# The last stage of an attention and expert layer: loops written out, and rows gathered four tiles ahead in place of eight

## Chip, cores and metric

The kernel runs on one core of a Trainium2 chip. The metric is the device time of one execution in microseconds (us); the time shown for a kernel is the median of several runs. One further execution was recorded by the hardware profiler, and the rows below come from it.

## What is computed

A layer norm of `x` (2 x 2048 x 512, float32) feeds two branches whose results are added to `x`. One is attention with 16 heads and a latent of 128; the other sends each token to 2 of 8 experts and takes the mean of their two results.

```python
x = L0_attn_x                                   # (2, 2048, 512)
xn = _layernorm(x, axis=-1)
x = x + attn(xn, ...) + ffn(xn, ...)
# attn ends with: out = o @ Wo.T + bo           (o: heads side by side, after Wo_h)
# ffn:
gate_logits = jnp.einsum('nsd,de->nse', x, gate_w) + gate_b
_, top_idx = jax.lax.top_k(gate_logits, K)      # K = 2 of E = 8
all_out = jax.nn.relu(jnp.einsum('nsd,edo->nseo', x, expert_w) + expert_b)
sel = jnp.take_along_axis(all_out, top_idx[..., None], axis=2)
return sel.mean(axis=2)
```

## The kernel before

The program is written engine by engine: SyncE, GpSimd (POOL), ScalarE (ACT), VectorE (DVE) and TensorE (PE) each have a list of instructions, and semaphores alone set the order between them. A helper `count(n)` adds 4 to a count because most semaphores start at 4.

The stages are: weights folded together; layer norm, queries, keys, values and gate logits, tile by tile (a tile is 128 tokens, `NT` = 32 tiles); attention, two heads per turn of a loop; then the experts. The tokens are sorted by expert into `PT` = 72 tiles of rows. For each, POOL gathers the token rows, PE multiplies them with the chosen expert's weights, DVE adds the biases, and SyncE writes the result to a table in device memory, `y_dram` (called `expert_rows` in the trace).

The last stage begins when the 72 expert tiles are done. It works on the 32 token tiles in order. Tile `n` uses slot `q = n % 8` of a ring of `OUT_RING` = 8 slots; each slot has one PSUM bank `PS[:, q]`, one residual buffer `xc[q]`, two buffers for gathered rows `y_g[q][0]` and `y_g[q][1]`, and one result buffer `acc[q]`. In the trace `y_g` is called `w_hi` or `w_lo` and `acc` `w_lo`, after the memory that they reuse, and `xc` is called `arena`.

- PE, `project` (line 1457): 12 matmuls (4 blocks of rows times 3 products of fp16 halves) give the attention output of one tile in bank `q`. The first 8 tiles are straight code; tiles 8 to 31 run in a loop of 3 turns with 8 tiles in the body. From tile 8 on it waits until DVE has read the same bank's previous tile.
- POOL (lines 739 to 749): straight code before and after. It waits until the whole expert table is written, then makes two indirect DMAs per tile, 128 rows of 512 float32 each (line 746), from the table into `y_g[q]`. For `n >= 8` the pair waits for `acc_done` of tile `n - 8`.
- DVE, `sums` (lines 1199 to 1208): a loop of 4 turns with 8 tiles in the body. It waits for the slot's previous result to be out (`out_done`, line 1202), for the residual (`xc_in`, line 1203), for the projection (`proj_ps`, line 1204), and adds projection and residual (line 1205); it waits for the gathered rows (`yg_in`, line 1206) and adds the two (lines 1207 and 1208). The last of these raises `acc_done`.
- SyncE: `result` (line 543) waits for `acc_done` and writes 128 x 512 float32 out; `residual` (line 537) loads `xc[q]` for the tile eight further on. The residual loads of tiles 0 to 7 are issued during the expert stage. A loop of 3 turns holds 8 results and 8 loads; the results of tiles 24 to 31 are straight code.

All instructions of a loop that name tile `m * 8 + q` take their addresses and counts from registers, which further register instructions fill.

Of the kernel before, what the change touches and what calls it, by code (L numbers as in the profile page):

```python
# [7 lines left out]
def layer_kernel(nc, x, Wq, Wdkv, Wuk, Wuv, ln_g, ln_b, Wo_h, Wo, bo,  # L8
# [30 lines left out]
    NT = B * ST  # L39
# [21 lines left out]
    with ctx:  # L61
# [3 lines left out]
        def sem(name):  # L65
            return ctx.enter_context(nc.semaphore(name))
# [32 lines left out]
        def carve(arena):  # L99
            at = [0]  # L100

            def take(n, dt=f32):
# [85 lines left out]
        tD = carve(arena2)  # L188
        xg_T = [tD(2 * KB * P, f16).rearrange("p (z k c) -> p z k c", z=2, k=KB) for _ in range(2)]
        y_sb = [tD(E) for _ in range(2)]  # L190
        OUT_RING = 8
        xc = [tD(E) for _ in range(4)]
        x_ahead = [tD(E).bitcast(f16) for _ in range(2)]
        xc += [tD(E) for _ in range(2)]
# [3 lines left out]
                 for w in (w_hi, w_lo) for q in range(NE * KB * E // (2 * E))]  # L198
        y_g, acc = [spare[TOP * q:TOP * (q + 1)] for q in range(OUT_RING)], spare[TOP * OUT_RING:TOP * OUT_RING + OUT_RING]
        x_g = [x_g0[:, :]] + x_ahead  # L200
# [3 lines left out]

        OUT_SEMS = [f"{name}{q}" for name in ("xc_in", "out_done", "yg_in") for q in range(OUT_RING)]
        s = {n: sem(n) for n in (
# [23 lines left out]
        START = 4  # L230
        FROM_ZERO = ["id_zero", "id_done", "ids_in", "xg_in0", "xg_in1", "xg_in2", "xg_in3"] + OUT_SEMS[-OUT_RING:]

        def count(n):

            return n + START
# [136 lines left out]
        def _(sp):  # L374
# [161 lines left out]
            def residual(m, q):  # L536
                sp.dma_start(xc[q], xc_v[q % B][ds(m * (OUT_RING // B) + q // B, 1)].rearrange("t p d -> (t p) d")
                             ).then_inc(s[f"xc_in{q}"], 16)

            def result(m, q):  # L540
                sp.wait_ge(s["acc_done"], count(m * OUT_RING + q + 1))
                sp.sem_inc(s["step_at"], 1)
                sp.dma_start(out_v[q % B][ds(m * (OUT_RING // B) + q // B, 1)].rearrange("t p d -> (t p) d"), acc[q]
                             ).then_inc(s[f"out_done{q}"], 16)

            def expert_rows(i):
                for u in range(2):
                    sp.wait_ge(s["y_done"], count(i * 2 + u + 1))
                    sp.dma_start(y_dram[ds((i * 2 + u) * P, P), :], y_sb[u]).then_inc(s[f"y_st{u}"], 16)
# [10 lines left out]
                residual(0, q)  # L560
            with sp.Fori(BESIDE + 5 + OUT_RING, PT // 2) as i:
                expert_rows(i)
            with sp.Fori(0, NT // OUT_RING - 1) as m:
                for q in range(OUT_RING):
                    result(m, q)
                    residual(m + 1, q)
# [7 lines left out]
        def _(pool):  # L574
# [165 lines left out]
                pool.wait_ge(s[f"y_st{u}"], count(16 * PT // 2))  # L740
            for n in range(NT):
                q, at = n % OUT_RING, n // B + n % B * ST
                if n >= OUT_RING:
                    pool.wait_ge(s["acc_done"], count(n - OUT_RING + 1))
                for k in range(TOP):
                    g.indirect_dma_start(out=y_g[q][k], out_offset=None, in_=y_dram,  # L746
                                         in_offset=bass.IndirectOffsetOnAxis(ap=place[:, k, at:at + 1], axis=0)
                                         ).then_inc(s[f"yg_in{q}"], 16)
# [154 lines left out]
        def _(dve):  # L903
# [264 lines left out]
            for it in range(ROUTING_ITS):  # L1168
                for kk in SPAN:
                    heads(it, True, [kk])  # L1170
                    if kk % 2 == 0:
                        n = next(steps)
# [26 lines left out]
            def sums(m, q):  # L1199
                n = m * OUT_RING + q  # L1200
                lnk, cnt = linker(dve, s["dveE"], n * 2)
                dve.wait_ge(s[f"out_done{q}"], count(m * 16))
                dve.wait_ge(s[f"xc_in{q}"], count((m + 1) * 16))
                dve.wait_ge(s["proj_ps"], count(n + 1))
                lnk(v.scalar_tensor_tensor(out=acc[q], in0=PS[:, q, :], scalar=1.0 / WS, in1=xc[q], op0=ALU.mult, op1=ALU.add))
                dve.wait_ge(s[f"yg_in{q}"], (m + 1) * (16 * TOP))
                lnk(v.tensor_tensor(acc[q], acc[q], y_g[q][0], ALU.add))
                v.tensor_tensor(acc[q], acc[q], y_g[q][1], ALU.add).then_inc(s["acc_done"], 1)

            with dve.Fori(0, NT // OUT_RING) as m:  # L1210
                for q in range(OUT_RING):
                    sums(m, q)

# [2 lines left out]
        def _(pe):  # L1216
# [234 lines left out]
            def project(m, q, again):  # L1451
                u, at = q % B, q // B * P
                if again:
                    pe.wait_ge(s["dveE"], count((m * OUT_RING + q - OUT_RING) * 2 + 1))
                terms = [(k, z, y) for k in range(KB) for z, y in pairs]
                for q_, (k, z, y) in enumerate(terms):
                    last = t.matmul(PS[:, q, :], attnT[:, u * KB + k, ds(m, 1), z, at:at + P].rearrange("p o q -> p (o q)"),  # L1457
                                    comb_hl[:, y, k, :], start=q_ == 0, stop=q_ == len(terms) - 1)
                last.then_inc(s["proj_ps"], 1)

            for q in range(OUT_RING):
                project(0, q, False)
            with pe.Fori(1, NT // OUT_RING) as m:
                for q in range(OUT_RING):
                    project(m, q, True)

# [24 lines left out]
```

## Time and profile before

| | us |
|---|---|
| median of 3 runs | 1613.08 |
| lowest and highest | 1612.5, 1616.36 |
| the profiled execution | 1613.21 |
| its span, first to last instruction | 1611.5 |
| PE busy | 1512.8 (94%) |
| DVE busy | 1137.4 (71%) |
| ACT busy | 902.2 (56%) |
| POOL busy | 583.6 (36%) |

Times within a profile are counted from the start of the span. A timeline row reads: start, duration, engine, source line, operation, what it writes and reads, how many instructions were merged, and in brackets how long the engine sat idle before it and what released it; "issue" means that nothing which the profile shows was waited for, "remote" that no releasing instruction of the trace was found. PEld is PE's weight load, an engine name ending in q its sequencer (register, branch and DMA-issuing instructions).

### The profile page before, as it was taken

What the parts mean: (1) busy time and instruction counts of PE and PEld (TensorE: products, weight loads), DVE (VectorE), ACT (ScalarE), POOL (GpSimd) and SP (SyncE); (2) the same over time, 40 slices, a digit from 0 to 9 for tenths busy, and PEclk for the clock granted to TensorE, in tenths of its full rate; (3) what the DMA queues carried; (4) which work ended last, traced back from release to release, by engine and by line L of the source; (5) the groups of instructions that cost most, each with busy time, mean ns of one, the idle gap of its engine ahead of it and who ended that gap; (6) DMA issues with size and microseconds to landing.
All of it is one profiled execution on the core that took longest, in us unless ns stands there. A gap on an engine that the chain in (4) does not pass through costs nothing.

```text
span 1611.5 us, 44000 instructions
## 1 busy us (share of the span) xinstructions
PE 1512.8 (94%) x12544; PEld 809.9 (50%) x12545; DVE 1137.4 (71%) x2384; ACT 902.2 (56%) x1629; POOL 583.6 (36%) x788
## 2 busy tenths in 40 slices
PE   5799989999999999999999999999999899999697
PEld 2788844444444444454444444444444455555233
DVE  5788778887777777777777777777777244444366
ACT  1677746666666666666666666666666433332000
POOL 2444402323454454432232223222322543332653
PEclk9899979999999999999999999999999999999798
DMA  6588851223222322233223322232232466554787
GB/s 161 164 268 271 236 151 52 72 67 93 71 69 62 90 77 70 64 83 84 70 63 81 85 70 63 81 86 70 63 78 63 135 207 217 177 174 142 253 280 250
DMA packets 161456, 198.05 MB, mean 123 GB/s; under 512 B 45792, under 2 KB 95072, under 8 KB 161024
## 3 DMA queue, kind: packets, MB, share of 16 engines
q1 hardware_dynamic: 125088, 117.11, 24.9%
q10 hardware_dynamic: 23328, 44.60, 9.4%
q0 software_dynamic: 12992, 35.77, 7.4%
q8 instruction: 21, 0.34, 0.1%
q14 instruction: 27, 0.22, 0.0%
HBM read 109.13 MB, written 63.12 MB: 107 GB/s over the span
## 4 chain that ended last, share of the span: by engine, by line
PE 79%; DVE 8%; issue 5%; DMA 3%; SPq 2%; ACT 1%; POOL 1%; DVEq 0%; ACTq 0%; POOLq 0%
PE PS L1328 29%; PE PS L1383 28%; PE PS L1433 12%; PE PS L1457 5%; DVE pm L1122 4%; PE PS L1415 2%; DMA arena<-in_x 1%; SPq L423 1%; DVE mx L1127 1%; SPq L415 1%; DVE mx L1126 1%; DVE arena L988 0%; PE PS L1274 0%; DMA q_pieces<-w_hi 0%; DMA arena<-in_Wuv 0%
## 5 line engine op out<-in xcount | busy, mean ns | idle before, releaser
L1122 DVE TENSOR_REDUCE pm<-PS 128x1 f32<-128x512 f32 (+3 forms) x1280 | 717.0, 602 | 200.3 <-PE PS L1328 185.3
L871 ACT ACTIVATE arena<-PS 128x512 f32<-128x512 f32 (+1 forms) x1152 | 613.5, 574 | 300.0 <-PE PS L1328 277.9
L1328 PE MATMUL PS<-arena 97*64 97x512 f16 (+7 forms) x5120 | 693.5, 353 | 26.6 <-DVE pm L1122 20.3
L1383 PE MATMUL PS<-arena 128*33 128x512 f32 (+3 forms) x2560 | 634.7, 531 | 1.9 <-POOL arena L649 1.9
L1328 PEld LDWEIGHTS PS<-arena 96*64 96x64 f16 (+1 forms) x5120 | 329.3, 110 | 416.3 <-DVE pm L1122 140.1
L649 POOL TENSOR_SCALAR_AFFINE_SELECT arena<-arena 128x256 f32<-128x256 f32 (+1 forms) x256 | 111.5, 436 | 546.7 <-ACT arena L871 545.6
L1383 PEld LDWEIGHTS PS<-arena 128*33 128x33 f32 x2560 | 159.4, 111 | 81.5 <-POOL arena L649 2.6
L1433 PE MATMUL PS<-w_hi,arena 128*128 x576 | 172.5, 381 | 0.7 <-issue 0.7
L890 ACT ACTIVATE arena<-PS 128x1024 f16<-128x1024 f32 x72 | 73.8, 1024 | 143.5 <-PE PS L1415 141.4
L1328 PE MATMUL PS<-later,deny 128*64 128x128 f16 x1024 | 145.4, 222 | 0.0
L1186 DVE SCALAR_TENSOR_TENSOR arena<-PS,eb_bc 128x512 f32<-128x512 f32 x72 | 49.8, 692 | 114.8 <-PE PS L1433 111.3
L1457 PE MATMUL PS<-comb_hl,arena 128*128 128x512 f16 x384 | 94.1, 400 | 22.9 <-issue 22.7
L1433 PE MATMUL PS<-w_lo,arena 128*128 x288 | 109.9, 382 | 0.0
L880 ACT ACTIVATE arena<-PS 97x512 f32<-97x512 f32 x128 | 76.5, 597 | 57.7 <-PE PS L1383 40.9
L1328 PEld LDWEIGHTS PS<-later,deny 128*64 128x64 f16 x1024 | 75.9, 112 | 57.1 <-issue 23.7
L746 POOL DMA_INDIRECT w_hi<-expert_rows,place x64 | 65.7, 1026 | 55.1 <-DMA expert_rows<-arena 21.7
L674 POOL TENSOR_TENSOR w_hi<-x_g,ws_col 128x512 f32 (+1 forms) x32 | 33.5, 1048 | 135.4 <-DVE bv_bc L1143 135.4
L1433 PEld LDWEIGHTS PS<-w_hi,arena 128*128 128x128 f16 x576 | 53.6, 98 | 53.0 <-issue 2.5
L1457 PEld LDWEIGHTS PS<-comb_hl,arena 128*128 (+1 forms) x384 | 38.4, 101 | 78.6 <-issue 40.0
L638 POOL DMA_INDIRECT token_of_place<-token_id,place_at x64 | 63.1, 986 | 16.4 <-issue 15.2
L688 POOL DMA_INDIRECT arena<-xn_rows,cur_id x54 | 52.6, 975 | 43.8 <-POOL cur_id L685 39.8
L621 POOL TENSOR_TENSOR arena<-arena 128x512 f16<-128x512 f32 x32 | 37.4, 1170 | 70.2 <-ACT arena L786 70.2
(174 smaller groups left out, 1296.8 us busy)
## 6 DMA issues: line engine op xcount, KB each, us to landing
expert_rows<-arena SPq DMA_DIRECT2D x72, 256.0 KB
comb_hl<-arena SPq DMA_DIRECT2D x256, 64.0 KB
arena<-q_pieces ACTq DMA_DIRECT2D x90, 128.0 KB
arena<-k_pieces ACTq DMA_DIRECT2D x90, 128.0 KB
v_rows<-w_lo SPq DMA_DIRECT2D x8, 1056.0 KB, 7.5
arena<-in_x SPq DMA_DIRECT2D x16, 512.0 KB, 5.7
xn_rows<-arena SPq DMA_DIRECT2D x16, 512.0 KB, 6.1
q_pieces<-w_hi SPq DMA_DIRECT2D x32, 256.0 KB, 5.3
```

Source lines behind the costliest of these rows:

```text
L638: g.indirect_dma_start(out=id_dram, out_offset=bass.IndirectOffsetOnAxis(ap=place_at[:, k, i:i + 1], axis=0), in_=token_id[:, i:i + 1], in ...
L649: g.affine_select(out=both[:, :, 0:wm], in_=both[:, :, 0:wm], compare_op=ALU.is_ge, fill=nought, base=0, pattern=[[step, 2], [1, wm]], cha ...
L688: g.indirect_dma_start(out=x_g[q], out_offset=None, in_=xn_dram, in_offset=bass.IndirectOffsetOnAxis(ap=cur_id[:, q:q + 1], axis=0)).then_ ...
L746: g.indirect_dma_start(out=y_g[q][k], out_offset=None, in_=y_dram, in_offset=bass.IndirectOffsetOnAxis(ap=place[:, k, at:at + 1], axis=0)) ...
L871: a.activation(probs[kk % 4][:, a_ * CH:a_ * CH + w], PS[:, s2_bank(k, x), 0:w], ACT.Exp, scale=SCALE).then_inc(s["exp_done"], 1)
L880: a.activation(ot[q % 2][0:2 * HD + V1, :], PS[0:2 * HD + V1, 6 + q % 2, :], ACT.Copy).then_inc(s["ot_done"], 1)
L890: a.activation(xg_T[u].rearrange("p z k c -> p (z k c)"), PS[:, 4 + 2 * u:6 + 2 * u, :].rearrange("p z c -> p (z c)"), ACT.Copy).then_inc( ...
L1122: v.reduce_max(pm[:, c, r, p:p + 1], PS[:, S1_BANK[n], 0:w], AX).then_inc(s["s1_done"], 1)
L1328: last = t.matmul(PS[h:h + P // 2, bank, cols], lhsT[:, h:h + P // 2], rhs, start=start, stop=stop)
L1383: last = t.matmul(PS[rows_, 6 + c % 2, CH - wds[a]:CH], v_sb[pu % 2][:, j + a, :], probs[pk % 4][:, a * off:a * off + wds[a]], start=p_ in ...
L1433: last = t.matmul(PS[:, u, :], xg_T[u][:, z, k, :], w[:, ds(e, 1), k * E:(k + 1) * E].rearrange("p e c -> p (e c)"), start=q_ == 0, stop=q ...
L1457: last = t.matmul(PS[:, q, :], attnT[:, u * KB + k, ds(m, 1), z, at:at + P].rearrange("p o q -> p (o q)"), comb_hl[:, y, k, :], start=q_ = ...
```

## The change

Two things change. On SyncE, DVE and PE the three loops of the last stage become Python loops, so that all 32 tiles (24 on PE, after the 8 that were straight already) are written out with constant addresses and counts. And a new constant `GATHERS_AHEAD` = 4 takes the place of the ring's 8 in POOL's wait: the gathers of tile `n` now wait for the sums of tile `n - 4`, from tile 4 on. Rings, buffers, transfers and arithmetic stay.

```diff
-        OUT_RING = 8
+        OUT_RING, GATHERS_AHEAD = 8, 4
@@ SyncE
-            with sp.Fori(0, NT // OUT_RING - 1) as m:
+            for m in range(NT // OUT_RING - 1):
                 for q in range(OUT_RING):
                     result(m, q)
                     residual(m + 1, q)
@@ POOL
             for n in range(NT):
                 q, at = n % OUT_RING, n // B + n % B * ST
-                if n >= OUT_RING:
-                    pool.wait_ge(s["acc_done"], count(n - OUT_RING + 1))
+                if n >= GATHERS_AHEAD:
+                    pool.wait_ge(s["acc_done"], count(n - GATHERS_AHEAD + 1))
                 for k in range(TOP):
                     g.indirect_dma_start(out=y_g[q][k], out_offset=None, in_=y_dram,
@@ DVE
-            with dve.Fori(0, NT // OUT_RING) as m:
+            for m in range(NT // OUT_RING):
                 for q in range(OUT_RING):
                     sums(m, q)
@@ PE
             for q in range(OUT_RING):
                 project(0, q, False)
-            with pe.Fori(1, NT // OUT_RING) as m:
+            for m in range(1, NT // OUT_RING):
                 for q in range(OUT_RING):
                     project(m, q, True)
```

## Rows read from the trace of the kernel before

**Rows 1.** The page: busy tenths of TensorE in 40 equal slices of the span.
```profile
PE   5799989999999999999999999999999899999697
```

**Rows 2.** Groups of instructions, 1488 to 1612: xcount, busy, mean ns, idle before, releasers.
```profile
L746 POOL DMA_INDIRECT w_hi<-expert_rows,place x64 | 65.7, 1026 | 55.1 <-DMA expert_rows<-arena 21.7 <-issue 19.2 <-DVE w_lo L1208 14.2
...
L1205 DVE SCALAR_TENSOR_TENSOR w_lo<-PS,arena 128x512 f32<-128x512 f32 x32 | 21.9, 685 | 42.0 <-remote 35.3 <-PE PS L1457 6.7
```

**Rows 3.** Timeline of TensorE in the last stage.
```profile
1488.44 21.62 PE L1457 MATMUL PS<-comb_hl,arena 128*128 128x512 f16 x98 [0.94 <-issue]
...
1531.70 0.58 PE L1457 MATMUL PS<-comb_hl,arena 128*128 128x512 f16 x1 [2.21 <-issue]
1533.11 18.12 PE L1457 MATMUL PS<-comb_hl,arena 128*128 128x512 f16 x71 [0.82 <-issue]
...
1553.71 16.78 PE L1457 MATMUL PS<-comb_hl,arena 128*128 128x512 f16 x77 [0.36 <-issue]
...
1576.48 28.02 PE L1457 MATMUL PS<-comb_hl,arena 128*128 128x512 f16 x116 [1.71 <-issue]
```

**Rows 4.** Timeline of VectorE: tiles 0, 2, then 6, 8, 12, 19, 25.
```profile
1498.67 0.69 DVE L1207 TENSOR_TENSOR w_lo<-w_lo,w_hi 128x512 f32<-128x512 f32 x1 [6.75 <-DMA w_hi<-expert_rows,place]
...
1506.27 0.69 DVE L1207 TENSOR_TENSOR w_lo<-w_lo,w_hi 128x512 f32<-128x512 f32 x1 [2.77 <-DMA w_hi<-expert_rows,place]
...
1533.86 0.69 DVE L1205 SCALAR_TENSOR_TENSOR w_lo<-PS,arena 128x512 f32<-128x512 f32 x1 [14.86 <-remote]
...
1537.97 0.69 DVE L1205 SCALAR_TENSOR_TENSOR w_lo<-PS,arena 128x512 f32<-128x512 f32 x1
...
1553.70 0.69 DVE L1205 SCALAR_TENSOR_TENSOR w_lo<-PS,arena 128x512 f32<-128x512 f32 x1 [6.46 <-remote]
...
1577.24 0.69 DVE L1205 SCALAR_TENSOR_TENSOR w_lo<-PS,arena 128x512 f32<-128x512 f32 x1 [8.94 <-remote]
...
1594.29 0.69 DVE L1205 SCALAR_TENSOR_TENSOR w_lo<-PS,arena 128x512 f32<-128x512 f32 x1 [4.54 <-PE PS L1457]
```

**Rows 5.** Stretches: length, busy and xcount of PE, PEld, DVE, ACT, POOL; PEclk, DMA share, GB/s.
```profile
1520.00:1532.00 12.00, 3.23 (x6) 0.62 (x6) 0.00 (x0) 0.00 (x0) 7.93 (x9) 0.50 0.88 282
1536.00:1544.00 8.00, 8.00 (x34) 3.42 (x33) 7.63 (x12) 0.00 (x0) 6.21 (x6) 0.88 0.79 258
1544.00:1552.00 8.00, 7.60 (x34) 3.05 (x32) 2.39 (x4) 0.00 (x0) 6.17 (x7) 1.00 0.99 367
```

**Rows 6.** Timeline of SyncE's queue: results out.
```profile
1500.32 0.69 SPq L543 DMA_DIRECT2D out<-w_lo  x1
...
1525.33 0.71 SPq L543 DMA_DIRECT2D out<-w_lo  x1
...
1536.25 0.33 SPq L543 DMA_DIRECT2D out<-w_lo  x1
```

**Rows 7.** Timeline of GpSimd: the first gather, those after a pause, the last.
```profile
1494.00 0.95 POOL L746 DMA_INDIRECT w_hi<-expert_rows,place  x1 [21.70 <-DMA expert_rows<-arena]
...
1536.27 0.95 POOL L746 DMA_INDIRECT w_hi<-expert_rows,place  x1 [5.89 <-DVE w_lo L1208]
...
1556.36 0.95 POOL L746 DMA_INDIRECT w_hi<-expert_rows,place  x1 [4.02 <-DVE w_lo L1208]
...
1579.65 0.95 POOL L746 DMA_INDIRECT w_hi<-expert_rows,place  x1 [4.26 <-DVE w_lo L1208]
...
1592.13 0.95 POOL L746 DMA_INDIRECT w_hi<-expert_rows,place  x1 [0.30 <-issue]
```

**Rows 8.** Single lines, TensorE's sequencer: ns min/median/max, first and last start.
```profile
L1457 PEldq FUSED_REGOPS  x192: 46/46/46, 1505.6 to 1600.0; - x192
...
L1463 PEldq COMPARE_BRANCH  x3: 76/207/209, 1553.9 to 1600.6; - x3
```

**Rows 9.** DMA queues between 1540 and 1544: kind, packets, MB, share of 16 engines.
```profile
q8 instruction: 1, 0.02, 1.7%
```

## Prediction

> **What bounds the kernel now.** I read the page first: TensorE (PE) is busy at 9 tenths in nearly every slice, but in the last three, where the touched stage lies, it has 6, 9 and 7 [rows 1]. Everything ahead keeps its time, so the sum is over that stage, from 1488.44 us, when the first projection matmul starts, to the end of the span at 1611.5.
>
> Then the stage by engine [rows 2]. Tiles are counted from 0. 32 tiles take four resources: PE 384 matmuls, in the straight part 98 of them in 21.62 us [rows 3], so some 2.65 us a tile and 85 us in all. VectorE (DVE) three operations a tile; its starts 1533.86 and 1537.97 are two tiles apart, so 2.06 us each and 66 us in all [rows 4]. GpSimd (POOL) two gathers a tile: 65.7 us busy and 19.2 us of gaps between them make 84.9 us, 1.33 us each [rows 2]. DMA 64 gathers, 32 results and 24 residual loads of 256 KB each, 31.5 MB; the fullest stretch moved 367 GB/s at a share of 0.99, which makes 86 us [rows 5]. So four floors lie between 66 and 86 us, and the stage takes 123.
>
> Where is the rest? DVE sat 42.0 us before its first sum of a tile, 35.3 of them "remote", and POOL 14.2 us behind DVE [rows 2]. In order of time: tile 6's first sum starts at 1533.86 after 14.86 us idle, tile 12's at 1553.70 after 6.46, tile 19's at 1577.24 after 8.94, tile 25's, which the trace puts down to PE, at 1594.29 after 4.54 [rows 4]. Of its waits (the ring's result out, the residual in, the projection) the first is met at once for tile 6 and the residual was loaded long ago; the projection is left. Yet PE had issued 98 matmuls by 1510.06, and tile 6 is complete with the 84th [rows 3]. From 1511 on PE issues a matmul every 1.4 or 2.1 us, 13 of them until 1531.70, though it waits for nobody ("issue"), and from 1533.11 it runs again, in the same moment as DVE [rows 3, 4]. SyncE's issues take 0.69 to 0.71 us each in this stretch and 0.33 after it [rows 6]. I read this as one thing, a **slow spell**: every instruction of PE and SyncE passes at one in some 0.7 us, and what PE has finished reaches DVE late. The lag is the same each time: 98 + 13 = 111 matmuls begun by 1531.7 against 84 released; 111 + 71 = 182 by 1551.2 against the 156 that tile 12 needs at 1553.70; 384 - 116 = 268 before 1576.48 against 240 for tile 19. That is 26 to 28 matmuls, over two tiles, and it explains why a spell is not felt at once.
>
> When do spells begin and end? They end when POOL stops: its pauses begin at 1530.4, 1552.3 and 1575.4 (start less idle time) and its last gather ends at 1593.1, and DVE is let go at 1533.86, 1553.70, 1577.24, 1594.29, that is 1.2 to 3.5 us later [rows 4, 7]. POOL stops only because its ring of 8 tiles is full: it had gathered tiles 0 to 13 and tile 14 wants the sum of tile 6. So the 14.86 us stall is long because POOL may run eight tiles ahead of a stalled DVE. Between 1520 and 1532 DVE did nothing at all, and the DMA share was still 0.88 [rows 5]. I can't show what a spell is, only its beginning under gathers and its end with them.
>
> **The change part by part.** (1) POOL waits for tile n-4 in place of n-8: the gathers of tiles 4 to 7 gain a wait too. POOL has nothing else queued, so only gathers stand behind it; DVE waits for those. Outside spells it costs nothing: a gather pair lands 2.5 to 4.9 us after its issue (at 1.25 us each from 1494.00, tile 0's pair is issued by 1496.2 and used at 1498.67, tile 2's by 1501.4 and used at 1506.27) [rows 4, 7]. Wait, two gathers, landing and two sums are 2.66 + 4.9 + 1.4 = 9.0 us for four tiles, 2.25 a tile, under POOL's own 2.66. If a landing took over 6.6 us this cover would be gone.
>
> In the first spell POOL may now go to tile 9, once tile 5 is summed, at 1519.0 (1533.86 less 14.86). With 28 gathers from 1494.00 to 1530.4, 1.3 us each, its 19th would be ready near 1517.4 to 1518; so 1.0 us idle, and the 20th ends by 1521.5. Then it waits for tile 6. The spell ends 1.2 to 3.5 us behind the gathers, as above, so at 1522.7 to 1525.0; with 2.1 us for tile 6's sums POOL restarts at 1524.8 to 1527.1. I take 4.2 us idle of 3.3 to 5.6. PE resumes some 10 us sooner than before.
>
> After it the same thing recurs. DVE ran 6, 7 and 6 tiles from one stall to the next (6, 12, 19, 25), and the lag of 26 to 28 matmuls in it doesn't depend on the ring. So I expect stalls near 12, 18 and 25, each with POOL idle for 4.0 to 5.9 us (three rows: 5.89, 4.02, 4.26 [rows 7]); I take 4.2 again.
>
> The ledger of POOL, before: 1494.0 + 84.9 + 14.2 = 1593.1, and a tail of 18.4 us to 1611.5, because seven tiles (25 to 31) were gathered and not summed: 7 x 2.06 after 1594.29, is 1608.7, then the last result's way out to 1611.5, 2.7 us. After: 1494.0 + 84.9 + 1.0 + 4.2 + 3 x 4.2 = 1596.7; the tail is short, since at most four tiles can be unsummed: landing 2.5 to 4.9 (3.7), two sums 1.4, way out 2.7, so 7.8 us. End of span 1604.5. So POOL is idle 3.6 us longer and the tail is 10.6 us shorter: **minus 7.0 us**. What is late next is POOL, then a stalled DVE.
>
> (2) The loops written out. PE loses 8 register instructions a tile (192 x 46 ns = 8.8 us), but a loop stretch had 77 matmuls in 16.78 us, 0.218 each, the straight part 98 in 21.62, 0.221: hidden, so nothing [rows 3, 8]. Three branches on PE are 76 to 209 ns each, 0.6 us at most, and at each PE is tiles ahead of DVE [rows 8]. DVE's tile keeps three operations of 0.69 us (685 ns the first; three such are 2.06, and 2.06 is its pitch), so its register steps are hidden; I take 0 [rows 2, 4]. SyncE loses a register step and a move for each of 48 transfers; if they take 0.7 us each in a spell, as its issues do [rows 6], results and residual loads leave up to 2.8 us a tile sooner there. Nobody waits for them (a residual is wanted eight tiles later), but more traffic falls into the spell. Taken at 0, with 0 to +1 us for each of four spells.
>
> Does straight code have to be fetched? An instruction packet came between 1540 and 1544 [rows 9], and PE was busy 8.00 of 8.00 us from 1536 to 1544 [rows 5]: that one cost nothing. The Trainium skill ("Runtime: NRT & Kernel Launch", section "Instruction fetch mechanics") says that code is streamed ahead in order and that a taken branch to a page outside the window makes the engine wait for a fetch, and so it speaks for writing loops out. The branches here show nothing of such a wait: DVE goes from tile 6 over the loop's end to tile 8 at its usual pitch. By that rule the loops' removal could only gain; by the row it gains nothing, and the sum has nothing of it.
>
> Sum: 1611.5 - 7.0 = 1604.5 for the span. The profiled execution took 1613.21, 1.7 more than its span and 0.1 over the median 1613.08. **Forecast 1606.2.**
>
> **The rivals.** *Spells rarer or gone.* Before, DVE left a stall with a full ring and ran at 2.06 us a tile, faster than POOL gathers: 0.5 MB of results and residuals in that time, beside the gathers, and the share reached 0.99 in 1544 to 1552 [rows 5]. With four tiles in hand it soon falls to POOL's 2.66. Against it: the first spell is there with DVE at POOL's pace (SyncE's issue took 0.69 us at 1500.32 already [rows 6]). With no spell: 1494.0 + 84.9 + 7.8 = 1586.7, time 1588.4; with two of four left, some 1597. Chance 0.20.
>
> *The gain given back.* If spells outlast the gathers by the 3.5 us of the first one rather than 1.2, or a fifth comes near tile 29, POOL's idle grows: four pauses of 5.9 in place of 4.2 add 6.8 us, so 1613; one further spell adds 4 to 6. Chance 0.15, times 1609 to 1616. This is also the case in which the change does nothing that it seems to: the new wait then only moves idle time from DVE to POOL.
>
> *Slower: code that comes late.* Straight code is new to PE, DVE and SyncE at each step, where the loop bodies were run again from what was there. Its packets queue with gathers at a DMA share of 0.9 and more. If they are not asked for early enough, each costs up to a landing, 4.9 us. PE's code of the stage grows from 16 tiles (8 straight, 8 in the loop) to 32, DVE's fourfold; I estimate 3 to 5 more packets from that, 15 to 25 us, less 7. It decides from 12 us (three late ones) upward: 1618 to 1624, 1621 in the middle. For: the DMA traffic; against: the packet of 1540 to 1544, and that a stalled engine also lets the queues drain. Chance 0.13.
>
> **How the numbers follow.** My forecast has 0.52, with a range of its own of 1600 to 1611 (idle 3.3 to 5.6 at the first, 4.0 to 5.9 at the others, landing 2.5 to 4.9, a spell less by luck). The measurement tells apart about 0.3%, 4.8 us, so bounds 1608.2 and 1617.9. Of the 0.52, 0.36 lies below 1608.2. Faster 0.36 + 0.20 = 0.56; same 0.16 + 0.11 = 0.27; slower 0.04 + 0.13 = 0.17. The range 1589 to 1616 leaves out the late code (0.13) and a few hundredths at either end of the others.
>
> **What would show it.** Right: DVE's "remote" wait before tile 6 ends at 1523 to 1525, not 1533.9; POOL shows four pauses behind DVE of 4 to 6 us in place of three, the last gather starts near 1596, the last sum follows it by 5 us, and SyncE's issues still take 0.7 us in stretches. Spells gone: no "remote" waits, DMA near 350 GB/s throughout. Late code: PE or DVE idle with "issue" while SyncE's issues are short, and instruction packets at these places. The forecast is wrong in its mechanism if a spell does not end with POOL's pause, or if pauses come every two or three tiles.

## The result, and the profile after

| | before | changed |
|---|---|---|
| median, us | 1613.24 (4 runs) | 1602.56 (4 runs) |
| lowest to highest | 1612.5 to 1616.36 | 1600.42 to 1605.32 |
| profiled execution: time, span | 1613.21, 1611.5 | 1605.32, 1603.6 |

The ratio is 0.9929, 95% interval 0.9911 to 0.9947: 11 us faster, on that chip. Which chip this first comparison ran on is not noted; on the chip of the next four experiments the kernel before takes 1612.9 us (22 runs), so the two are taken to be one, the **first chip**. On two other chips, met later by chance, the kernel before takes 1589 to 1591 us by itself, and no kernel timed beside it there differs from it by more than 0.1%; the changed kernel itself was not timed on them. The experiments come to that.

The page of the changed kernel, busy tenths of TensorE, answers [rows 1]: the last three slices are 8, 8 and 7.

```profile
PE   5799989999999999999999999999999999999887
```

The groups of the stage, from 1480 us to the end (answer to [rows 2]; busy and mean, then idle before and releasers):

```profile
L746 POOL DMA_INDIRECT w_hi<-expert_rows,place x64 | 66.0, 1031 | 54.5 <-DMA expert_rows<-arena 21.6 <-issue 18.0 <-DVE w_lo L1208 14.9
...
L1207 DVE TENSOR_TENSOR w_lo<-w_lo,w_hi 128x512 f32<-128x512 f32 x32 | 22.1, 692 | 20.7 <-DMA w_hi<-expert_rows,place 17.4 <-issue 2.7
L1205 DVE SCALAR_TENSOR_TENSOR w_lo<-PS,arena 128x512 f32<-128x512 f32 x32 | 21.9, 684 | 23.9 <-remote 21.2 <-PE PS L1457 2.7
```

DVE's "remote" waits fell from 35.3 to 21.2 us. POOL's pauses behind DVE didn't fall: 14.9 after 14.2. The timeline of DVE shows where its waits are now, at tiles 6, 7, 17 and 26 (answer to [rows 4]; before, they were at 5, 6, 12, 19 and 25):

```profile
1521.23 0.69 DVE L1205 SCALAR_TENSOR_TENSOR w_lo<-PS,arena 128x512 f32<-128x512 f32 x1 [4.61 <-remote]
...
1527.66 0.69 DVE L1205 SCALAR_TENSOR_TENSOR w_lo<-PS,arena 128x512 f32<-128x512 f32 x1 [4.29 <-remote]
...
1558.96 0.69 DVE L1205 SCALAR_TENSOR_TENSOR w_lo<-PS,arena 128x512 f32<-128x512 f32 x1 [6.05 <-remote]
...
1587.35 0.69 DVE L1205 SCALAR_TENSOR_TENSOR w_lo<-PS,arena 128x512 f32<-128x512 f32 x1 [6.27 <-remote]
```

The timeline of TensorE (answer to [rows 3]): long runs of matmuls, and between them single ones or a few at a time, some 0.3 to 1.1 us apart with nothing waited for.

```profile
1490.63 23.47 PE L1457 MATMUL PS<-comb_hl,arena 128*128 128x512 f16 x108 [0.94 <-issue]
...
1516.14 0.38 PE L1457 MATMUL PS<-comb_hl,arena 128*128 128x512 f16 x1 [1.05 <-issue]
...
1526.08 26.78 PE L1457 MATMUL PS<-comb_hl,arena 128*128 128x512 f16 x119 [0.37 <-issue]
...
1558.84 23.31 PE L1457 MATMUL PS<-comb_hl,arena 128*128 128x512 f16 x100 [0.33 <-issue]
```

What these "remote" waits wait for stands in the trace too, among its semaphore events, though the timeline names no releaser. `proj_ps` is the count that the last matmul of each tile raises. In the kernel before it is raised at 1533.83, 1533.96 and 1534.08 us, three times within 0.26 us, at the end of the stall of tile 6, and again three times in 0.25 to 0.27 us from 1553.67, 1577.22 and 1594.27. In the changed kernel the threes begin at 1527.53, 1558.84 and 1587.23. Three tiles are 36 matmuls, and one takes 0.216 us where they run on, so the last two of the three were multiplied earlier: their signals were held back and came out together. On the chips without such stalls `proj_ps` is raised every 2.59 us. (The traces of the first chip hold 22 to 30 of 33 of its events, those of the others all, so no signal's delay is measured by itself.)

The timeline of GpSimd (answer to [rows 7]): the first gather, the first one after each pause, the last one.

```profile
1496.10 0.94 POOL L746 DMA_INDIRECT w_hi<-expert_rows,place  x1 [21.61 <-DMA expert_rows<-arena]
...
1523.64 0.94 POOL L746 DMA_INDIRECT w_hi<-expert_rows,place  x1 [1.20 <-DVE w_lo L1208]
...
1530.07 0.95 POOL L746 DMA_INDIRECT w_hi<-expert_rows,place  x1 [4.23 <-DVE w_lo L1208]
...
1561.37 0.94 POOL L746 DMA_INDIRECT w_hi<-expert_rows,place  x1 [4.62 <-DVE w_lo L1208]
...
1589.77 0.94 POOL L746 DMA_INDIRECT w_hi<-expert_rows,place  x1 [4.83 <-DVE w_lo L1208]
...
1594.00 0.95 POOL L746 DMA_INDIRECT w_hi<-expert_rows,place  x1 [0.31 <-issue]
```

So the ledger of POOL (first gather, plus busy time and gaps between gathers, plus pauses behind DVE, plus the tail from its last gather to the end of the span) reads 1496.1 + 84.0 + 14.9 + 8.6 = 1603.6, against 1494.0 + 84.9 + 14.2 + 18.4 = 1611.5 before. The stage began 2.1 us later in this execution; counted from the first gather it is 10.0 us shorter, and 9.8 of that is the tail. This profiled execution is the slowest of the four, 2.8 us over their median.

### The profile page after: what moved, and what is told of

Its sections match the earlier page's. It is cut to its first block, busy times and chain, and to the rows that moved or that the text cites. A ratio compares the mean times of both kernels' runs of the same rounds, so it can differ in the third digit from the quotient of the medians.

```text
span 1603.6 us, 43541 instructions
## 1 busy us (share of the span) xinstructions
PE 1514.2 (94%) x12544; PEld 811.6 (51%) x12545; DVE 1136.6 (71%) x2384; ACT 902.1 (56%) x1629; POOL 583.4 (36%) x788
## 4 chain that ended last, share of the span: by engine, by line
PE 78%; DVE 9%; issue 4%; DMA 4%; SPq 2%; ACT 1%; POOL 1%; another core or an unknown queue 0%; DVEq 0%; ACTq 0%; POOLq 0%
PE PS L1328 28%; PE PS L1383 28%; PE PS L1433 12%; PE PS L1457 5%; DVE pm L1122 5%; PE PS L1415 2%; DMA arena<-in_x 1%; DVE mx L1127 1%; DMA q_pieces<-w_hi 1%; SPq L423 1%; SPq L415 1%; DVE mx L1126 1%; DVE arena L988 0%; PE PS L1274 0%; DMA bv_bc<-inverses 0%
## 5 line engine op out<-in xcount | busy, mean ns | idle before, releaser
L1328 PEld LDWEIGHTS PS<-arena 97*64 97x64 f16 (+1 forms) x5120 | 330.1, 110 | 417.5 <-DVE pm L1122 136.0
L674 POOL TENSOR_TENSOR w_hi<-x_g,ws_col 128x512 f32 (+1 forms) x32 | 33.5, 1047 | 137.0 <-DVE bv_bc L1143 137.0
L1457 PEld LDWEIGHTS PS<-comb_hl,arena 128*128 128x128 f16 x384 | 38.5, 101 | 68.8 <-issue 29.3
```

Source lines behind the costliest of these rows:

```text
L1328: last = t.matmul(PS[h:h + P // 2, bank, cols], lhsT[:, h:h + P // 2], rhs, start=start, stop=stop)
```

## The experiments

The first question was which half of the change brings the gain. Theory A is the prediction's: a spell lasts as long as POOL gathers, so the depth of its lead is all. Theory B is that the register and branch instructions of the loops are what is slow.

**One part alone: four ahead, loops kept.**

```diff
 # before.py
-        OUT_RING = 8
+        OUT_RING, GATHERS_AHEAD = 8, 4
-                if n >= OUT_RING:
-                    pool.wait_ge(s["acc_done"], count(n - OUT_RING + 1))
+                if n >= GATHERS_AHEAD:
+                    pool.wait_ge(s["acc_done"], count(n - GATHERS_AHEAD + 1))
```

> The loops stay, only the gathers wait for tile n-4. Theory A (the forecast's: a slow spell lasts as long as the gathers run, the ring's depth decides how long, loops cost nothing): the whole gain is here, 1600 to 1605 us, tile 6's first sum starts near 1523 and not 1534, four pauses of GpSimd. Theory B (the register and branch instructions of the loops are what is slow in a spell): little gain, 1610 to 1613.

Measured: 1605.9 us, ratio 0.9955 (0.9938 to 0.9972), so 7.0 us of the gain. The first row is the group of gathers, then DVE's timeline with the waits of 4 us and more, at tiles 5, 11, 18 and 24:

```profile
L746 POOL DMA_INDIRECT w_hi<-expert_rows,place x64 | 66.7, 1042 | 55.6 <-DMA expert_rows<-arena 20.8 <-issue 18.0 <-DVE w_lo L1208 16.8
```

```profile
1517.68 0.69 DVE L1205 SCALAR_TENSOR_TENSOR w_lo<-PS,arena 128x512 f32<-128x512 f32 x1 [7.08 <-remote]
...
1537.56 0.69 DVE L1205 SCALAR_TENSOR_TENSOR w_lo<-PS,arena 128x512 f32<-128x512 f32 x1 [4.56 <-remote]
...
1560.43 0.69 DVE L1205 SCALAR_TENSOR_TENSOR w_lo<-PS,arena 128x512 f32<-128x512 f32 x1 [5.04 <-PE PS L1457]
...
1580.37 0.69 DVE L1205 SCALAR_TENSOR_TENSOR w_lo<-PS,arena 128x512 f32<-128x512 f32 x1 [5.35 <-remote]
```

This is the forecast's picture: stalls 6 or 7 tiles apart, four pauses of POOL of 4.0 to 4.4 us (16.8 in all), and a tail of 8.5 us (1492.0 + 84.7 + 16.8 = 1593.5, span 1602.0). The stall of 14.86 us is gone. The median is 0.9 us above A's 1600 to 1605 and 4 below B's 1610 to 1613, and it isn't the whole gain, as A had it: nearer to A, but neither.

**The other part alone: straight code, eight ahead.**

```diff
 # after.py
-        OUT_RING, GATHERS_AHEAD = 8, 4
+        OUT_RING, GATHERS_AHEAD = 8, 8
```

> All loops written out, but the gathers wait for tile n-8 as before. Theory A: as before within 3 us, 1610 to 1615, with a stall of VectorE of some 15 us at tile 6 or 7 and a tail of some 18 us behind the last gather. Theory B: most of the gain, 1601 to 1606.

Measured: 1607.6 us, ratio 0.9966 (0.9953 to 0.998), 5.3 us faster. Neither theory had that. A's shape is there (a stall of 13.34 us at tile 7, a tail of 1609.5 - 1590.9 = 18.6 us), but the median is 2.4 us below A's range: with eight ahead, straight code is worth about 5 us on this chip. With four ahead it is worth 3.3 to 3.7 (1605.9 less 1602.6 or 1602.2). The group shows pauses of 11.5 us where the loops had 14.2, and DVE's timeline the long stall. This profiled execution is the slowest of eleven (1611.2 us), so it shows less of the gain than the median:

```profile
L746 POOL DMA_INDIRECT w_hi<-expert_rows,place x64 | 65.3, 1020 | 51.2 <-DMA expert_rows<-arena 21.1 <-issue 18.6 <-DVE w_lo L1208 11.5
```

```profile
1538.30 0.69 DVE L1205 SCALAR_TENSOR_TENSOR w_lo<-PS,arena 128x512 f32<-128x512 f32 x1 [13.34 <-remote]
```

The two parts alone give 7.0 and 5.3 us, together 10.7 against the 12.3 of their sum; with intervals of plus or minus 2 to 3 us on each, that they add up is not excluded.

**Other depths, straight code.**

```diff
 # after.py
-        OUT_RING, GATHERS_AHEAD = 8, 4
+        OUT_RING, GATHERS_AHEAD = 8, 3      # the other kernel: 8, 6
```

> Straight code, gathers wait for tile n-3. Theory A: spells end sooner, but two gathers (2.6), landing (up to 4.9) and two sums (1.4) make 9 us for three tiles, 3.0 a tile against 2.6 of GpSimd's own, so VectorE waits for rows: 1600 to 1610, about the time of four ahead. If landing is nearer 2.5 than 4.9 there is no such wait and the time is 1598 to 1601. Theory B: the same time as four ahead, 1602.

> Straight code, gathers wait for tile n-6. Theory A: half way between eight and four: the first stall ends some 5 us later than with four (GpSimd runs two tiles further), the tail is up to two tiles longer: 1605 to 1609. Theory B: 1602, no dependence on the depth.

Measured: three ahead 1602.9 us, ratio 0.9933 (0.9912 to 0.9954); six ahead 1607.5, ratio 0.9966 (0.9954 to 0.9979). Depth 3 and 4 are the same, 6 and 8 are the same (1607.5 and 1607.6), with the step between 4 and 6. Theory B, for which the depth is nothing, is out; for three ahead both theories allowed the time. For six ahead the profiled execution suggests why: its last long stall came at tile 26, when POOL had done everything, so the tail was 17.5 us (1494.1 + 83.6 + 10.9 = 1588.6, span 1606.1). Three ahead is the telling one. Its groups, then TensorE's timeline after 1520 us:

```profile
L746 POOL DMA_INDIRECT w_hi<-expert_rows,place x64 | 65.3, 1020 | 54.6 <-DMA expert_rows<-arena 21.1 <-issue 18.9 <-DVE w_lo L1208 14.6
L1207 DVE TENSOR_TENSOR w_lo<-w_lo,w_hi 128x512 f32<-128x512 f32 x32 | 22.2, 694 | 41.1 <-DMA w_hi<-expert_rows,place 36.3 <-issue 4.1 <-DVE w_lo L1205 0.3
L1205 DVE SCALAR_TENSOR_TENSOR w_lo<-PS,arena 128x512 f32<-128x512 f32 x32 | 21.9, 684 | 2.3 <-PE PS L1457 2.3
```

```profile
1520.66 54.55 PE L1457 MATMUL PS<-comb_hl,arena 128*128 128x512 f16 x252 [0.59 <-issue]
```

No "remote" wait is left, and 252 matmuls run through at 0.216 us each. Yet the time is that of four ahead, because POOL now pauses nine times for 0.8 to 2.7 us, 14.6 us in all, and DVE waits 36.3 us for rows. The spells' cost was turned into the cost of a lead too short for the landing time, at the same price.

These kernels also show that POOL's stop is what ends a spell. In straight code the first spell ends, that is TensorE's next long run of matmuls begins, 25.9 us after the first gather with three ahead, 30.0 and 33.5 with four (two profiled executions), 36.3 with six and 42.0 with eight. Each time it is 1.6 to 3.6 us after POOL has begun to wait for the first time.

**Which loop?** The next kernels were to tell apart TensorE's loop from the others', and its register instructions from its branches, and whether less traffic ends the spells.

```diff
 # f1_pe_straight: after.py with the loops of SyncE and VectorE put back
 # f2_pe_loop: after.py with TensorE's loop put back
 # f3_straight_regs: after.py with
+            nought = pe.value_load(zero_ids[0:1, 0:1], min_val=0, max_val=1)
-                    last = t.matmul(PS[:, q, :], attnT[:, u * KB + k, ds(m, 1), z, at:at + P] ...
+                    last = t.matmul(PS[:, q, :], attnT[:, u * KB + k, ds(m - z_, 1), z, at:at + P] ...
                     # z_ is 0 for tiles 0 to 7 and the register nought for tiles 8 to 31
 # f4_no_reload: after.py without residual(m + 1, q), and
-                dve.wait_ge(s[f"xc_in{q}"], count((m + 1) * 16))
+                dve.wait_ge(s[f"xc_in{q}"], count(16))
```

> Gathers four ahead; TensorE's code straight, the loops of VectorE and SyncE kept. Theory C (TensorE's own instructions decide how soon a spell is felt: 8 register steps a tile more in the loop, so the stall comes after 6 or 7 tiles and not after 9 or 10): as the changed kernel, 1601 to 1604 us, stalls 9 or 10 tiles apart. Theory E (the loops of SyncE and VectorE are what costs): as with all loops kept, 1605 to 1607.

> Gathers four ahead; only TensorE keeps its loop, VectorE and SyncE have straight code. Theory C: as with all loops kept, 1605 to 1607, stalls 6 or 7 tiles apart. Theory E: 1601 to 1604, stalls 9 or 10 tiles apart.

> As the changed kernel, but TensorE's addresses go through a register that holds zero, so that the straight code has the loop's 8 register steps a tile and no branch. Theory C (the register steps): 1605 to 1607 and stalls 6 or 7 tiles apart. Theory D (the branches, or code fetched again behind them): as the changed kernel, 1601 to 1604, stalls 9 or 10 tiles apart.

> As the changed kernel without the 24 residual loads of the stage (tiles 8 to 31 add the residual of tiles 0 to 7 again, so the result differs): 25.2 MB in place of 31.5. Theory L (spells come when the DMA engines are full, at a share of 0.99 and more): at GpSimd's pace the stage then needs some 300 GB/s, under the 367 to 410 of full engines, so no spell or a short one, no remote wait of VectorE over 2 us, and the time is near GpSimd's own 84 us of gathers: 1587 to 1592. Theory G (spells come from a long run of gathers, whatever else is moved): stalls as before the edit, 1598 to 1603.

Measured: 1592.0, 1590.3, 1591.0 and 1590.2 us, where the kernel before took **1590.1** (31 runs). The ratios are 1.001 (0.9996 to 1.0023), 1.0006 (0.9992 to 1.0019), 1.0001 (0.9991 to 1.0011) and 1.0003 (0.9993 to 1.0013). These runs were on another chip than the first ones, and on it none of the four profiles has a spell. TensorE's timeline of the kernel in which it keeps its loop, and a stretch of the kernel in which only its loop is written out (columns as in [rows 5]):

```profile
1487.31 83.04 PE L1457 MATMUL PS<-comb_hl,arena 128*128 128x512 f16 x384 [0.94 <-issue]
```

```profile
1540.00:1580.00 40.00, 36.35 (x169) 16.29 (x167) 30.46 (x47) 0.00 (x0) 30.56 (x32) 1.00 1.03 396
```

All 384 matmuls in one run, over three turns of a loop. In the other kernel they take 83.04 us too, without a pause, until 1576.35, under 396 GB/s at a share of 1.03. So these four could not tell their theories apart; what they show is that without spells the loops cost nothing and a depth of four costs nothing against eight.

**The kernel before, profiled without spells.** No edit.

> The kernel before, unchanged, profiled again, because it took 1590.1 us on one chip and 1612.9 on another. If this chip has slow spells: 1610 to 1616, VectorE waits remote at tiles 5 or 6, 12, 19, and TensorE's 384 matmuls take over 100 us. If it has none: 1586 to 1594, all 384 matmuls in one run of 83 us, no remote wait, no pause of GpSimd behind VectorE.

Measured on a third chip: 1591.1 us, where other runs of the same kernel beside it had a median of 1588.9 (ratio 1.0009, 0.9996 to 1.0022). TensorE's timeline, the groups and two stretches (length, busy and count of the engines, granted clock, DMA share, GB/s):

```profile
1489.36 83.04 PE L1457 MATMUL PS<-comb_hl,arena 128*128 128x512 f16 x384 [0.94 <-issue]
```

```profile
L746 POOL DMA_INDIRECT w_hi<-expert_rows,place x64 | 68.5, 1070 | 40.3 <-DMA expert_rows<-arena 21.1 <-issue 19.2
...
L1205 DVE SCALAR_TENSOR_TENSOR w_lo<-PS,arena 128x512 f32<-128x512 f32 x32 | 21.8, 683 | 2.2 <-PE PS L1457 2.2
```

```profile
1500.00:1540.00 40.00, 40.00 (x187) 18.14 (x186) 26.87 (x41) 0.00 (x0) 31.16 (x30) 1.00 0.98 350
1540.00:1580.00 40.00, 32.40 (x151) 14.45 (x148) 29.87 (x45) 0.00 (x0) 31.16 (x30) 0.95 1.01 368
```

Set beside [rows 2 to 4], which are the same kernel on the first chip: no "remote" wait in place of 35.3 us, no pause of POOL in place of 14.2. POOL's ledger is 1494.4 + 87.7 + 0 + 8.3 = 1590.4, so POOL bounds the stage, and the ring of eight leaves no long tail because DVE never falls behind. And the DMA engines are full for 80 us (share 0.98 and 1.01) under an unbroken run of 64 gathers. So neither full engines nor a long run of gathers is enough for a spell on this chip.

**Less traffic, once more.** The edit is that of the kernel without reloads above.

> The changed kernel without the 24 residual loads of the stage once more (25.2 MB in place of 31.5, tiles 8 to 31 add the residual of tiles 0 to 7 again). On a chip with spells: theory L (spells come when the DMA engines are full) 1587 to 1594 and no remote wait over 2 us; theory G (a long run of gathers is enough) 1598 to 1603 with remote waits of 4 us and more. On a chip without spells: as the kernel before within 2 us.

Measured on that same third chip: 1589.9, ratio 1.0005 (0.9995 to 1.0015). Without spells a fifth less traffic gains nothing, as a stage bound by POOL's issue would have it. Whether it would end spells where there are some stays untried, since both runs fell on chips without them.

**The change itself and the register steps, once more.** The last two, the changed kernel without an edit and the one with the zero register once more, fell on the first chip again.

> The changed kernel, unchanged, timed again. On a chip without slow spells the wait on tile n-4 never binds for long and the loops cost nothing, so it is as the kernel before within 2 us (ratio 0.999 to 1.001), at 1587 to 1593. On a chip with spells it is 0.991 to 0.995 of the kernel before, as first measured.

> The changed kernel with TensorE's addresses through a register that holds zero (8 register steps a tile, no branch), once more. On a chip with spells: theory C (the register steps bring the stalls closer together) 1605 to 1607 and stalls 6 or 7 tiles apart; theory D (the branches and code behind them) 1601 to 1604 and 9 or 10 tiles apart. On a chip without spells: as the kernel before within 2 us.

Measured: the changed kernel 1602.2 us, ratio 0.9932 (0.9905 to 0.9959), as the first time (0.9929). Its profiled execution has three stalls, at tiles 8, 16 and 25 (that of tile 16, of 3.7 us, ends 0.2 us before POOL begins to wait), and the ledger 1493.9 + 84.9 + 12.6 + 7.9 = 1599.3. TensorE's runs in it:

```profile
1527.36 26.08 PE L1457 MATMUL PS<-comb_hl,arena 128*128 128x512 f16 x105 [0.82 <-issue]
1553.67 20.45 PE L1457 MATMUL PS<-comb_hl,arena 128*128 128x512 f16 x94 [0.23 <-issue]
```

With the register steps put back into straight code: 1601.9 us, ratio 0.9939 (0.992 to 0.9959), the kernel before being at 1611.9. TensorE's sequencer has the 192 register steps of [rows 8], and the timeline the runs between stalls:

```profile
L1457 PEldq FUSED_REGOPS  x192: 46/46/90, 1504.3 to 1583.5; - x192
```

```profile
1519.23 21.07 PE L1457 MATMUL PS<-comb_hl,arena 128*128 128x512 f16 x88 [1.53 <-issue]
...
1542.75 21.05 PE L1457 MATMUL PS<-comb_hl,arena 128*128 128x512 f16 x89 [0.32 <-issue]
...
1567.65 20.33 PE L1457 MATMUL PS<-comb_hl,arena 128*128 128x512 f16 x92 [1.03 <-issue]
```

The time is theory D's (no cost of TensorE's register steps), the stalls (tiles 6, 13, 21, 29) are 7 or 8 apart and lie between the two theories. TensorE's runs from one stall to the next are 69 to 75 matmuls with all loops, 88 and 89 with its register steps alone (the 92 go on to the end), 119 and 100 in the changed kernel's first profile and 105 and 94 in its second. So, as far as so few profiles tell, the register steps bring stalls closer, by about half the difference, but that cost no time that can be measured. What straight code gains in the rest (branches, or the loops of SyncE and VectorE) is open: the kernels that would split it ran where there was nothing to split.

## Why the prediction came out as it did

The forecast was 1606.2 and the measured median 1602.6. The span was forecast as 1604.5 and is 1603.6, but that nearness is in part luck: the stage began 2.1 us later in this execution. From the first gather on the forecast has 110.5 us, and the two profiles of the changed kernel have 107.5 and 105.4. The kernel with its loops kept has 110.0, with 16.8 us of pauses and a tail of 8.5 for the forecast's 17.8 and 7.8, and takes 1605.9. So the forecast is right for the shorter lead, and what it is off by is the straight code.

- *Spells, their lag, their end with POOL's pause.* Right on this chip. Lag: tile 17 needs 216 matmuls and is let go at 1558.96; TensorE had begun 120 + 119 = 239 by 1552.9 (120 by 1526.08) and 247 by then, so the lag is 31. Counted at that moment the prediction's three are 29, 31 and 30, not 26 to 28; that it is nearly the same each time holds. POOL's pauses begin at 1525.8, 1556.8 and 1584.9, and DVE is let go at 1527.66, 1558.96 and 1587.35, 1.8 to 2.4 us later. Not every wait of DVE ends so. Tile 6 of the changed kernel is let go at 1521.23, 1.2 us before POOL's next pause, and tile 5 of the kernel before at 1516.85, with POOL running on to 1530.4: single matmuls that pass in a spell let a tile go too. What came back only with POOL's stop is TensorE's full pace.
- *The first stall.* Forecast: POOL stops after tile 9, tile 6 is let go at 1522.7 to 1525.0, which is 1524.8 to 1527.1 with this execution's start. Measured 1521.23 for tile 6, in the middle of the spell, with 4.29 us more for tile 7, let go at 1527.66: two stalls of 8.9 us in place of one of 14.86 and one of 4.26 (that of tile 5, 1516.85 less 1512.6).
- *The tail.* Forecast 7.8, measured 8.6 (18.4 before). It is the largest of the terms that change and carries nearly all of the gain in the profiled execution.
- *POOL's pauses.* Forecast 1.0 + 4.2 + 3 x 4.2 = 17.8, measured 14.9: each is the size forecast (4.23, 4.62, 4.83, and 1.20 for the short one), but there are three long ones, not four, since stalls came at 17 and 26 rather than at 12, 18 and 25. With the loops kept they came at 5, 11, 18 and 24 and the pauses sum to 16.8: there the forecast's count holds.
- *The loops, priced at nothing.* This step failed. Straight code alone brought 5.3 us, and 3.3 to 3.7 on top of four ahead, which is the distance from the forecast to the median. The argument that register steps and branches lie hidden is true outside spells (384 matmuls in 83.04 us with and without the loop), but I read it from stretches without a spell and used it for spells. SyncE's issues of 0.7 us need both a spell and loop code. In the loop of the kernel before the results' issues take 0.69 to 0.71 us in the first spell, some 0.01 or 0.09, and 0.33 behind it [rows 6]; on the third chip, in the same loop, those of tiles 0 to 23 take 0.33 or 0.34. In the straight code of the changed kernel they take 0.33 us throughout, also in the stretch 1544 to 1557 at whose end TensorE stalls. The stretch (columns as in [rows 5]) and SyncE's timeline of the changed kernel (answer to [rows 6]):

```profile
1544.00:1557.00 13.00, 10.28 (x46) 4.31 (x45) 6.81 (x11) 0.00 (x0) 10.01 (x10) 1.00 1.03 401
```

```profile
1550.10 0.33 SPq L543 DMA_DIRECT2D out<-w_lo  x1
...
1553.00 0.33 SPq L543 DMA_DIRECT2D out<-w_lo  x1
```

  So "every instruction of PE and SyncE passes at one in some 0.7 us" was too wide, and "SyncE's issues still take 0.7 us" didn't come.
- *The rivals.* "Spells rarer" is in part what happened, three for four, by straight code and not by the shorter lead (four with the loops kept and four tiles ahead, three in straight code with six and with eight). "Spells gone" is what two other chips show of every kernel, the one before included: 1589 to 1591 against its 1588.4.
- *Late code.* It was not seen: on the second chip TensorE ran 384 straight matmuls in 83.04 us at a DMA share of 0.96 to 1.03. One of its signs was there, though: in the spell after 1552.9 us TensorE idles with "issue" while SyncE's issues are short. The other was not. The changed kernel has no instruction packet in any of its three spells, and TensorE is back at full pace at 1526.08 and 1558.84, before the packets of 1530 and 1561.5. In all it has five such packets in the stage, the kernel before three: two more, not three to five. (The rival's time was also added up wrongly: 15 to 25 us less 7 on 1613.1 is 1621 to 1631, not 1618 to 1624.) The Trainium skill ("Runtime: NRT & Kernel Launch", "Instruction fetch mechanics") names a taken branch out of the window of fetched pages as what makes an engine wait for a fetch. The traces show no such wait here: without spells TensorE takes 83.04 us with its loop kept or written out, and on the first chip the kernel before has no instruction packet between 1543 and 1609 us, where all three of TensorE's branches lie [rows 8]. So nothing in the traces puts the 5.3 us of straight code on the first chip down to fetched code, and no run there separates branches from the rest.

What stays open is what a spell is, and why straight code makes it cost less. The same kernel has spells on one chip and not on two others, at the same DMA share and under the same gathers. Held-back signals and POOL's stop as their end are shown; the cause is not.

## What to carry to other kernels

When two engines feed a third and one may run a ring ahead, its lead can cost twice if the third stalls for as long as the first works, as here: the stall lasts as long as the lead, and what has been gathered is worked off behind the last gather (a tail of 18.4 us with eight tiles, 8.6 with four). The lead has to cover landing time and little more: here six and eight tiles cost 5 us more than four, and three, too few to cover it, lost in waits for rows what they saved in stalls. And a wait without a releaser in the trace, in a stretch where an engine issues slowly for no reason shown, should be looked at on more than one chip before a change is tuned to it: the 7 us of the shorter lead and the 5 of straight code were not there in any kernel timed on the other two chips.

## What the runs showed of the hardware

- The kernel before takes 1611.9 to 1613.2 us on one chip and 1588.9 to 1591.1 on two others, some 1.4% less; the mean granted clock of the profiled executions is 0.975 and 0.979. All of it lies in the last stage, 117.5 us from the first gather in the one and 96.0 in the other.
- On the first chip TensorE at times issues one matmul in 0.7 to 2.8 us with nothing waited for, and a tile is let go to VectorE when 24 to 31 matmuls behind it stand in the trace as begun (waits of 4 us and more in seven profiles). The count that releases it is then raised three times in 0.26 us, where 36 matmuls need 7.8.
- There TensorE's next long run of matmuls begins about 1 to 3.6 us after GpSimd stops gathering, in nearly every spell and at every depth.
- On the other chips the DMA engines moved 368 and 396 GB/s at shares of 1.01 and 1.03 for 40 us with TensorE's matmuls in one unbroken run to their end; on the first chip 401 GB/s at 1.03 went with a stall.
- With a fifth less traffic the time on the other chips stays within 0.1% (1590.2 us for 1590.1, and 1589.9 for 1588.9).
